# Choosing the two experts of a token on VectorE: thirteen pieces of one operation instead of six pieces of two or three

## The chip, the core and the metric

One core of a Trainium2 chip. The metric is the device time of one execution in microseconds (us); lower is better. The engines are TensorE (PE; its weight loads are listed as PEld), VectorE (DVE), ScalarE (ACT), GpSimd (POOL) and SyncE (SP, which only issues DMAs). Each engine works through its own instructions in order, and waits for others, or for its own earlier results, on semaphores.

## The reference, cut to what matters

A transformer block on x of shape (4, 1024, 128): layer norm with modulation, attention with 16 heads of 8 features, a gated residual, a second modulated layer norm, and a mixture of 8 experts of which each token uses two, with another gated residual. The part that the change touches is the choice of the two experts:

```python
logits = jax.nn.silu(xt @ rw1 + rb1) @ rw2 + rb2
_, idx = jax.lax.top_k(logits, K)                     # K = 2 of E = 8
mask = jnp.zeros((n, E), bool).at[jnp.arange(n)[:, None], idx].set(True)
w = jax.nn.softmax(jnp.where(mask, logits, -jnp.inf), axis=1)
```

## The kernel before, in words

Three stages follow one another: `prepare` (first norm, q, k, v), `attend` (attention of all four sequences, and beside it the routing of the first three) and `mix` (the experts, and beside them the routing of the last sequence). Each is a block that all engines enter and leave together.

`attend` runs 256 steps, 64 for each sequence: 4 groups of 4 heads, 16 steps each, one step for 128 keys against 512 queries. Softmax subtracts the row maximum, so the scores are computed twice. In each step PE makes two *maximum units* (`max_scores`, L711: two products of 128x512 into one of two PSUM buffers `ps_max`); DVE reduces each unit to its row maxima (`take_max`, L902), and PE may write unit n only when unit n-2 has been reduced. PE also makes four score tiles (L732) which ACT turns into probabilities (L832), and adds the probabilities' products with v (`add_ctx`, L747, two halves per step). PE's order in a step is: first half of `add_ctx`, two score tiles, second half, first unit, two score tiles, second unit, then what else is due (`beside`). Every 8 steps DVE joins the maxima of a half group (`row_max`, L910), ACT copies the finished context (L837), PE transposes it (L768) and ACT copies it again (L844), and DVE inverts the sums (L917).

The routing of sequence b is laid out by hand over the 64 steps of the next sequence: `route_time(s)` gives b and the step n, and `ROUTE_AT` the steps of PE's and ACT's parts (the logits at n = 34 and 36, the counting matmul at 45). On DVE, `route_piece(s, place)` runs behind each unit of the step, at position `at = 2n + place`; below, a unit is named by that position (unit 75 is the second one of n = 37). The choice starts behind unit 75. It works on small tiles (128 partitions, 8 token tiles, 8 experts: 64 elements a partition): add the bias; then twice (n = 0, 1): maximum over the experts (`top`), which experts equal it (`cand[0]`), times a table of descending numbers (`cand[1]`), maximum of that (`first`), the one that equals it (`chosen`); in between the first choice is pushed down to -3e38 (`left`). At the end `both`, the sum of the two masks, for PE's counting matmul, and `gap`, the difference of the two maxima, for the weights.

Each operation but the last two goes through `link`: the operation raises a semaphore when it has finished, and DVE waits for it before it goes on.

```python
def link(ins):
    ins.then_inc(step, 1)
    dve.wait_ge(step, steps.more())
```

In `mix` DVE makes the same choice for the last sequence behind expert tiles 18 and 19. It copies there the weights of a tile (L1572) and adds the bias to its result (L1578).

Of the kernel before, what the change touches and what calls it, by code (L numbers as in the profile page):

```python
# [22 lines left out]
ALU = mybir.AluOpType  # L23
ACT = mybir.ActivationFunctionType
AX = mybir.AxisListType
# [53 lines left out]
W_UP, W_B1, W_B2, W_END = 0, HID, HID + HC, HID + HC + D  # L79
assert CLEARS * CLEAR == SLOT_TILES  # L80
PAD = 4
ROUTE = ("ctx0", "ctx1", "proj0", "proj1", "turn0", "turn1", "router0", "router1", "logits0", "logits1", "counts")


# [442 lines left out]
def attend(nc, t, k):  # L527
    with ExitStack() as ctx:
# [40 lines left out]
        r = route_buffers(k["routing"], sb, "_attend", spare[0], spare[1].rearrange("p (t d) -> p t d", d=D))  # L569
# [327 lines left out]
        @block.vector  # L897
        def _(dve):
            def take_max(n):
                g, u, tile, c = n // UNITS, n // 2 % 2, n % UNITS // 4, n % 2  # L900
                dve.wait_ge(max_scores_ready, n + 1)
                dve.reduce_max(half_max[tile // HT % 2][:, c, 2 * u:2 * u + 2, tile % HT],  # L902
                               ps_max[n % 2][:].rearrange("p (r n) -> p r n", r=2), axis=AX.X).then_inc(max_taken, 1)

            def join_halves(h):

                dve.wait_ge(max_taken, HALF_UNITS * (h + 1))
                if h:
                    dve.wait_ge(max_parts_ready, h)
                dve.tensor_tensor(row_max[:], half_max[h % 2][:, 0], half_max[h % 2][:, 1],  # L910
                                  ALU.max).then_inc(row_max_ready, 1)

            def invert_sums(chunk):

                dve.wait_ge(slot_taken, SLOT["turned", chunk] + 1)
                view = turned[chunk % 2][:].rearrange("p (t c) -> p t c", c=32)
                dve.reciprocal(inv_sum[chunk % 2][:], view[:, :, HD]).then_inc(sums_inverted, 1)  # L917

            def step(s):
                for place, n in enumerate(units(s)):  # L920
                    if n is not None:
                        take_max(n)
                    route_piece(s, place)
                if s and (chunk := turned_in(s - 1)) is not None:
                    invert_sums(chunk)
                if (h := split_in(s)) is not None:
                    join_halves(h)

            def route_piece(s, place):

                b, n = route_time(s)
                if not 0 <= b < EARLY:
                    return
                at = 2 * n + place
                if 26 <= at < 26 + NT:
                    route.stats(b, at - 26)
                if at == 26 + NT:
                    route.variance(b)
                if 75 <= at < 81:
                    if at == 75:  # L940
                        dve.wait_ge(slot_taken, SLOT["logits1", b] + 1)
                        if b:
                            dve.wait_ge(r.slot_ready, b)
                    route.choice(at - 75)
                if at == 98 and b == EARLY - 1:
                    dve.wait_ge(r.slot_ready, EARLY)
                    route.tiles(0)

            route = route_on_dve(dve, k, r)
            for n in range(HALF_UNITS):  # L950
                take_max(n)
            join_halves(0)
            for n in range(HALF_UNITS, HALF_UNITS + LEAD):
                take_max(n)
            join_halves(1)
            dve.wait_ge(r.tables_ready, r.TABLES)
            for s in range(ALL_STEPS):
                step(s)
            invert_sums(CHUNKS - 1)
# [10 lines left out]
def routing(nc, ctx, k):  # L970
# [25 lines left out]
    r.fold4, r.fold2 = sb("fold4", [P, 2, NT, NE // 2]), sb("fold2", [P, 2, NT, NE // 4])  # L996
    r.both = sb("both", [P, PAD + NT, NE])
    r.top = [sb(f"top{i}", [P, NT]) for i in range(2)]
# [250 lines left out]
def route_on_dve(dve, k, r):  # L1249

    step, steps = r.dve_step, r.dve_steps
# [5 lines that stand above are left out]
# [14 lines left out]
    wide = [P, NT, NE]  # L1271

    def over_e(v):
        return v[:].unsqueeze(2).to_broadcast(wide)

    def add_bias():
        link(dve.tensor_tensor(r.logit[:], r.logit_in[:], r.rb2[:].unsqueeze(1).to_broadcast(wide), ALU.add))

    def top(n):
        of = r.logit if n == 0 else r.left  # L1280
        link(dve.tensor_reduce(r.top[n][:], of[:], axis=AX.X, op=ALU.max))
        link(dve.tensor_tensor(r.cand[0][:], of[:], over_e(r.top[n]), ALU.is_equal))

    def first_of(n):

        link(dve.tensor_tensor(r.cand[1][:], r.cand[0][:], r.order[:].unsqueeze(1).to_broadcast(wide), ALU.mult))
        link(dve.tensor_reduce(r.first[n][:], r.cand[1][:], axis=AX.X, op=ALU.max))

    def choose(n):
        link(dve.tensor_tensor(r.chosen[:, n], r.cand[1][:], over_e(r.first[n]), ALU.is_equal))  # L1290
        if n == 0:
            link(dve.scalar_tensor_tensor(out=r.left[:], in0=r.chosen[:, 0], scalar=-3e38, in1=r.logit[:],
                                          op0=ALU.mult, op1=ALU.add))

    def both():
        dve.tensor_tensor(r.both[:, PAD:, :], r.chosen[:, 0], r.chosen[:, 1], ALU.add).then_inc(r.both_ready, 1)
        dve.tensor_tensor(r.gap[:], r.top[0][:], r.top[1][:], ALU.subtract).then_inc(r.gap_ready, 1)

    def choice(piece):

        n, part = divmod(piece, 3)
        if part == 0:
            if n == 0:
                add_bias()
            top(n)
        if part == 1:
            first_of(n)
        if part == 2:
            choose(n)
            if n == 1:  # L1310
                both()

    def tiles(stage):

# [23 lines left out]
        dve.tensor_scalar(r.expert[:, at:at + n], r.expert_f[:, 0:n], float(NE - 1), None,  # L1338
                          ALU.min).then_inc(r.tiles_ready, 1)

    made = Steps()
    made.choice = choice
    made.stats = stats
    made.variance = variance
    made.tiles = tiles
    return made


def route_on_pe(pe, k, r):
# [48 lines left out]
def mix(nc, t, k):  # L1398
# [5 lines left out]
    with ExitStack() as ctx:  # L1404
# [40 lines left out]
        r = route_buffers(k["routing"], sb, "_mix")  # L1445
# [114 lines left out]
        def _(dve):  # L1560
# [73 lines left out]
            for n in range(ALL_TILES):  # L1634
                later = n + WRING - 1
                add_bias(n)
                if later < ALL_TILES:
                    copy_w(later, e)
                if later + 1 < ALL_TILES:
                    e = expert(later + 1)  # L1640
                if n == 3:
                    dve.wait_ge(route_taken, ROUTE.index("proj1") + 1)
                    late.gate(LATE)
                if n == 4:
                    late.residual(LATE)
                if n == 5:
                    for tile in range(NT):
                        route.stats(LATE, tile)
                if n == 6:
                    route.variance(LATE)  # L1650
                if n in (8, 9):
                    late.norm(LATE, n - 8)
                if n == 10:
                    late.modulate(LATE)
                if n == 11:
                    late.shift(LATE)
                if n == 16:
                    late.update(LATE)
                if n == 18:
                    dve.wait_ge(route_taken, ROUTE.index("logits1") + 1)  # L1660
                    for piece in range(3):
                        route.choice(piece)
                if n == 19:
                    for piece in range(3, 6):
                        route.choice(piece)
                if n == 22:
                    dve.wait_ge(route_taken, ROUTE.index("counts") + 1)
                    places.slots(LATE, 1)
                if n == 24:
                    places.weights(LATE)  # L1670
                if n == 26:
                    route.tiles(1)
                for b, at in enumerate(COMBINE_AT):
                    if n == at:
                        weigh(b, 0, whole)
                    if n == at + 1:
                        weigh(b, 1, whole)
                    if n == at + 2:
                        add_choices(b, whole)
                    if n == at + 3:  # L1680
                        gate_sum(b, whole)
                    if n == at + 4:
                        add_to_x(b, whole, 2)
                if n in (GATED_AT, GATED_AT + 1):
                    gate_weight(n - GATED_AT)
            for half in range(2):
                part = slice(half * NT // 2, (half + 1) * NT // 2)
# [107 lines left out]
```

## Time and profile before

| | |
|---|---|
| median of 3 runs | 989.49 us (988.11 to 991.61) |
| the profiled execution | 991.75 us; its span 989.9 us |
| DVE busy | 779.0 us (79% of the span) |
| L902 alone | 596.3 us, 512 units of 1216 ns |
| ACT busy | 760.6 us (77%); L832 553.8 us |
| PE busy | 869.6 us (88%), granted clock 0.947 over the span |

The busy times of a page are an average over the three stages. Matmul ends are modelled, so PE's 88% doesn't say that PE is the limit. In `attend`, DVE, ACT and PE are all close to full, and which of them is waited for changes from step to step.

### The profile page before, as it was taken

The numbers are of one execution on the slowest core, as the hardware profiler recorded it, in microseconds if no ns is written. First come the engines' busy times: TensorE is split into PE (matmuls) and PEld (weight loads), VectorE is DVE, ScalarE is ACT, GpSimd is POOL, SyncE is SP. The second block draws the span as 40 slices with busy tenths as digits, with TensorE's granted clock in tenths as the row PEclk, the third lists the DMA queues.
The fourth block names the chain that finished last, engine by engine and source line by source line (L and its number), as shares of the span: only waits on it lengthen the run. The fifth ranks groups of instructions, "written<-read, shape, count | busy, mean of one in ns | idle before, by whom it ended". The sixth has DMA issues, their size and how long they took to land. (4 is left out here: it accounts for less than half of the span.)

```text
span 989.9 us, 22083 instructions
## 1 busy us (share of the span) xinstructions
PE 869.6 (88%) x7998; PEld 398.6 (40%) x7998; DVE 779.0 (79%) x1058; ACT 760.6 (77%) x1636; POOL 347.8 (35%) x649
## 2 busy tenths in 40 slices
PE   6554799999999999899999989999998869998991
PEld 3230133333333233233323323332332259998991
DVE  6949799999998988998898899989886117643385
ACT  5550399999999888899988889998888946665660
POOL 6522000000003352161235216133522616477573
PEclk9775599999999999999999999999999979999996
DMA  5672041441431010171001001100000112123553
GB/s 141 242 278 84 1 147 37 145 176 34 146 115 47 20 34 2 34 225 45 16 20 34 2 33 37 42 19 17 2 2 2 45 47 61 55 69 83 147 139 88
DMA packets 60394, 72.06 MB, mean 73 GB/s; under 512 B 9949, under 2 KB 42212, under 8 KB 60288
## 3 DMA queue, kind: packets, MB, share of 16 engines
q1 hardware_dynamic: 55456, 61.82, 19.3%
q0 software_dynamic: 4544, 8.44, 2.6%
q8 instruction: 66, 1.08, 0.5%
q10 hardware_dynamic: 288, 0.40, 0.1%
q14 instruction: 40, 0.33, 0.1%
HBM read 30.08 MB, written 41.06 MB: 72 GB/s over the span
## 5 line engine op out<-in xcount | busy, mean ns | idle before, releaser
L902 DVE TENSOR_REDUCE half_max<-ps_max 128x2 f32<-128x1024 f32 x512 | 596.3, 1216 | 62.2 <-PE ps_max L711 61.1
L832 ACT ACTIVATE probs<-ps_scores 128x512 f32<-128x512 f32 x1024 | 553.8, 596 | 71.8 <-PE ps_scores L732 57.5
L747 PE MATMUL ps_ctx<-probs,v_grp 128*32 128x256 f32 x4096 | 328.7, 393 | 13.2 <-ACT probs L832 12.4
L711 PE MATMUL ps_max<-k_set,q_set 48*128 48x512 bf16 x1024 | 207.4, 400 | 36.4 <-DVE half_max L902 29.3
L732 PE MATMUL ps_scores<-q_set,k_set 51*128 51x512 bf16 x1024 | 206.5, 386 | 0.7 <-DMA q_set<-max_rows 0.5
L747 PEld LDWEIGHTS ps_ctx<-probs,v_grp 128*32 128x32 f32 x4096 | 80.8, 108 | 141.2 <-issue 71.9
L711 PEld LDWEIGHTS ps_max<-k_set,q_set 48*128 48x128 bf16 x1024 | 49.9, 94 | 191.7 <-DVE half_max L902 105.7
L732 PEld LDWEIGHTS ps_scores<-q_set,k_set 51*128 51x128 bf16 x1024 | 73.1, 93 | 134.0 <-ACT probs L832 94.2
L1541 ACT ACTIVATE hid<-ps_up,w_tile 128x128 f32<-128x128 f32 x312 | 89.2, 368 | 48.1 <-PE ps_up L1708 48.0
L1509 POOL DMA_INDIRECT y_rows<-y,slots_in x78 | 90.0, 1154 | 64.6 <-DVE y L1578 48.7
L638 POOL CAST max_parts<-row_max 128x16 bf16<-128x16 f32 x32 | 6.3, 197 | 297.4 <-DVE row_max L910 297.1
L1708 PE MATMUL ps_up<-slots_t,w_tile 128*128 128x128 f32 x624 | 84.7, 280 | 2.3 <-DVE w_tile L1572 2.3
L1718 PE MATMUL ps_down<-w_down,hid 128*128 x624 | 83.0, 276 | 0.4 <-DVE y L1578 0.4
L1578 DVE TENSOR_TENSOR y<-ps_down,w_tile 128x128 f32<-128x128 f32 x78 | 22.7, 290 | 73.3 <-PE ps_down L1718 63.2
L1708 PEld LDWEIGHTS ps_up<-slots_t,w_tile 128*128 128x128 f32 x624 | 77.5, 195 | 3.6 <-DVE w_tile L1572 2.8
L1718 PEld LDWEIGHTS ps_down<-w_down,hid 128*128 128x128 f32 x624 | 75.9, 192 | 0.7 <-issue 0.6
L1145 POOL DMA_INDIRECT slots<-h,slot x64 | 62.9, 983 | 19.6 <-issue 16.2
L630 POOL TENSOR_TENSOR ctx<-turned,inv_sum 128x128 f32<-128x128 f32 x32 | 13.0, 406 | 126.1 <-DVE inv_sum L917 126.1
L1572 DVE COPY w_tile<-w_all 128x644 f32 x78 | 39.3, 504 | 6.5 <-issue 6.3
L1702 PE MATMUL ps_slots_t<-ident,slots_in 128*128 128x128 f32 x78 | 22.0, 283 | 13.5 <-DMA slots_in<-slots 13.5
L1536 ACT COPY slots_t<-ps_slots_t 128x128 f32<-128x128 f32 x78 | 21.8, 280 | 13.9 <-PE ps_slots_t L1702 13.9
L851 ACT COPY max_rows<-ps_scores 48x128 bf16<-48x128 bf16 x32 | 8.0, 251 | 25.8 <-PE ps_scores L760 25.8
(200 smaller groups left out, 625.7 us busy)
## 6 DMA issues: line engine op xcount, KB each, us to landing
slots<-zero_rows SPq DMA_DIRECT2D x43, 387.0 KB, 5.2
q_terms<-parts SPq DMA_DIRECT2D x24, 256.0 KB, 2.8
k_terms<-parts SPq DMA_DIRECT2D x24, 256.0 KB, 3.2
q_set<-q_terms SPq DMA_DIRECT2D x32, 192.0 KB
k_set<-k_terms SPq DMA_DIRECT2D x32, 192.0 KB
slots_in<-slots SPq DMA_DIRECT2D x78, 64.5 KB, 1.8
rows<-y_rows SPq DMA_DIRECT2D x16, 256.0 KB, 5.1
q_set<-max_rows SPq DMA_DIRECT2D x128, 3.0 KB
```

The source lines that it names most:

```text
L711: ins = pe.matmul(ps_max[n % 2][:, r * BANK:(r + 1) * BANK], q_set[g % SETS][rows, u, tile * P:(tile + 1) * P], k_set[g % SETS][rows, u, c ...
L732: pe.matmul(bank[:], k_set[g % SETS][operand, u, tile * P:(tile + 1) * P], q_set[g % SETS][operand, u, c * BANK:(c + 1) * BANK], start=Tru ...
L747: ins = pe.matmul(ps_ctx[32 * head:32 * head + 32, columns], v_grp[g % 2][:, tile, head, :], probs[:, s % RING, head, columns], start=tile ...
L832: act.activation(probs[:, s % RING, place, :], ps_scores[n % BANKS_S][:], ACT.Exp, scale=float(HD) ** -0.5).then_inc(slot_taken, 1)
L902: dve.reduce_max(half_max[tile // HT % 2][:, c, 2 * u:2 * u + 2, tile % HT], ps_max[n % 2][:].rearrange("p (r n) -> p r n", r=2), axis=AX. ...
L1145: pool.indirect_dma_start(k["slots"], bass.IndirectOffsetOnAxis(r.slot[:, b, n, i:i + 1], axis=0), r.h[:, i, :], None).then_inc(r.scattere ...
L1509: pool.indirect_dma_start(k["y_rows"], bass.IndirectOffsetOnAxis(to, axis=0), y[n % YRING][:], None, bounds_check=Y_ROWS - 1, oob_is_err=F ...
L1541: ins = act.activation(hid[n % 2][:, c, :], ps_up[n % 2][:, c * P:(c + 1) * P], ACT.Silu, bias=w_tile[n % WRING][:, W_B1 + c:W_B1 + c + 1])
L1572: dve.tensor_copy(w_tile[n % WRING][:], w_all[:, e, :]).then_inc(w_ready, 1)
L1578: dve.tensor_tensor(y[n % YRING][:], ps_down[n % 2][:, 0:D], w_tile[n % WRING][:, W_B2:W_END], ALU.add).then_inc(y_ready, 1)
L1708: ins = pe.matmul(ps_up[n % 2][:, c * P:(c + 1) * P], w_tile[n % WRING][:, c * P:(c + 1) * P], slots_t[n % 2][:], start=True, stop=True)
L1718: ins = pe.matmul(ps_down[n % 2][:, 0:D], hid[n % 2][:, c, :], w_down[:, e, c, :], start=c == 0, stop=c == HC - 1)
```

## The change

The choice becomes thirteen pieces, at positions 75 to 87. Each is one operation (the last has two), and the wait for an operation's result stands ahead of the next piece instead of right behind the operation. The result of each operation and their order are the same. In `mix` the first six pieces go behind tile 18 and the other seven behind tile 19, so that `left` moves from the former to the latter.

```diff
+CHOICES = 13
...
-                if 75 <= at < 81:
+                if 75 <= at < 75 + CHOICES:
...
-    def add_bias():
-        link(dve.tensor_tensor(r.logit[:], r.logit_in[:], r.rb2[:].unsqueeze(1).to_broadcast(wide), ALU.add))
-
-    def top(n):
+    def made(ins):
+
+        ins.then_inc(step, 1)
+        steps.more()
+
+    def choice(piece):
+
+        dve.wait_ge(step, steps.seen)
+        if piece == 0:
+            made(dve.tensor_tensor(r.logit[:], r.logit_in[:], r.rb2[:].unsqueeze(1).to_broadcast(wide), ALU.add))
+            return
+        n, part = divmod(piece - 1, 6)
         of = r.logit if n == 0 else r.left
-        link(dve.tensor_reduce(r.top[n][:], of[:], axis=AX.X, op=ALU.max))
-        link(dve.tensor_tensor(r.cand[0][:], of[:], over_e(r.top[n]), ALU.is_equal))
...
+        if part == 0:
+            made(dve.tensor_reduce(r.top[n][:], of[:], axis=AX.X, op=ALU.max))
+        if part == 1:
+            made(dve.tensor_tensor(r.cand[0][:], of[:], over_e(r.top[n]), ALU.is_equal))
+        if part == 2:
+            made(dve.tensor_tensor(r.cand[1][:], r.cand[0][:], r.order[:].unsqueeze(1).to_broadcast(wide), ALU.mult))
+        if part == 3:
+            made(dve.tensor_reduce(r.first[n][:], r.cand[1][:], axis=AX.X, op=ALU.max))
+        if part == 4:
+            made(dve.tensor_tensor(r.chosen[:, n], r.cand[1][:], over_e(r.first[n]), ALU.is_equal))
+        if part == 5 and n == 0:
+            made(dve.scalar_tensor_tensor(out=r.left[:], in0=r.chosen[:, 0], scalar=-3e38, in1=r.logit[:],
                                           op0=ALU.mult, op1=ALU.add))
...
+        if part == 5 and n == 1:
+            dve.tensor_tensor(r.both[:, PAD:, :], r.chosen[:, 0], r.chosen[:, 1], ALU.add).then_inc(r.both_ready, 1)
+            dve.tensor_tensor(r.gap[:], r.top[0][:], r.top[1][:], ALU.subtract).then_inc(r.gap_ready, 1)
...
-                    for piece in range(3):
+                    for piece in range(CHOICES // 2):
                         route.choice(piece)
                 if n == 19:
-                    for piece in range(3, 6):
+                    for piece in range(CHOICES // 2, CHOICES):
                         route.choice(piece)
```

On DVE, from the first operation of the choice of sequence 0 on, with what each instruction waits for (`route_dve_step` is the semaphore of `link`, `max_scores_ready` says that PE has filled a unit); before:

```order
L902 TENSOR_REDUCE half_max<-ps_max 128x2 [waits max_scores_ready] x4
L1277 TENSOR_TENSOR logit<-logit_in,rb 128x64 [waits score_slot_taken]
L1281 TENSOR_REDUCE top<-logit 128x8 [waits route_dve_step]
L1282 TENSOR_TENSOR cand<-logit,top 128x64 [waits route_dve_step]
L917 RECIPROCAL inv_sum<-turned 128x16 [waits score_slot_taken,route_dve_step]
L902 TENSOR_REDUCE half_max<-ps_max 128x2 [waits max_scores_ready]
L1286 TENSOR_TENSOR cand<-cand,order 128x64
L1287 TENSOR_REDUCE first<-cand 128x8 [waits route_dve_step]
L902 TENSOR_REDUCE half_max<-ps_max 128x2 [waits max_scores_ready,route_dve_step]
```

and at the same place in the changed kernel (its lines are numbered one or more higher):

```order
L903 TENSOR_REDUCE half_max<-ps_max 128x2 [waits max_scores_ready] x4
L1286 TENSOR_TENSOR logit<-logit_in,rb 128x64 [waits route_dve_step,score_slot_taken]
L918 RECIPROCAL inv_sum<-turned 128x16 [waits score_slot_taken]
L903 TENSOR_REDUCE half_max<-ps_max 128x2 [waits max_scores_ready]
L1291 TENSOR_REDUCE top<-logit 128x8 [waits route_dve_step]
L903 TENSOR_REDUCE half_max<-ps_max 128x2 [waits max_scores_ready]
L1293 TENSOR_TENSOR cand<-logit,top 128x64 [waits route_dve_step]
```

The units and the reciprocal no longer wait for an operation of the choice, and between an operation and the one that needs its result there now stands a unit. At the end of the same choice on DVE, before:

```order
L1290 TENSOR_TENSOR chosen<-cand,first 128x64
L1296 TENSOR_TENSOR both<-chosen 128x64 [waits route_dve_step]
L1297 TENSOR_TENSOR gap<-top 128x8
L902 TENSOR_REDUCE half_max<-ps_max 128x2 [waits max_scores_ready] x7
L910 TENSOR_TENSOR row_max<-half_max 128x16 [waits max_parts_ready,max_taken]
```

and in the changed kernel:

```order
L1299 TENSOR_TENSOR chosen<-cand,first 128x64 [waits route_dve_step]
L903 TENSOR_REDUCE half_max<-ps_max 128x2 [waits max_scores_ready]
L1304 TENSOR_TENSOR both<-chosen 128x64 [waits route_dve_step]
L1305 TENSOR_TENSOR gap<-top 128x8
L911 TENSOR_TENSOR row_max<-half_max 128x16 [waits max_parts_ready,max_taken]
```

The seven units that stood between the choice and the joining of the maxima (units 81 to 87) now stand between the choice's last operations, and `both` is made seven units later.

## Rows read from the trace of the kernel before

**Rows 1.** Busy time by window (columns named in the first line): choice group, regular group.

```profile
core 0: us, PE busy (x) PEld busy (x) DVE busy (x) ACT busy (x) POOL busy (x), PEclk, DMA share, GB/s
387.40:411.10 23.70, 20.59 (x210) 7.04 (x208) 21.60 (x34) 18.88 (x38) 1.24 (x5) 1.00 0.04 12
...
140.00:159.80 19.80, 19.46 (x203) 6.21 (x200) 18.80 (x19) 18.55 (x37) 1.25 (x5) 1.00 0.22 70
```

**Rows 2.** Timeline of DVE, choice of sequence 0: start us, us, instruction, [idle before].

```profile
391.59 2.36 DVE L902 TENSOR_REDUCE half_max<-ps_max 128x2 f32<-128x1024 f32 x2 [1.45 <-PE ps_max L711]
393.86 0.21 DVE L1277 TENSOR_TENSOR logit<-logit_in,rb 128x64 f32<-128x64 f32 x1
394.11 0.22 DVE L1281 TENSOR_REDUCE top<-logit 128x8 f32<-128x64 f32 x1
...
396.37 1.23 DVE L902 TENSOR_REDUCE half_max<-ps_max 128x2 f32<-128x1024 f32 x1
...
402.69 0.22 DVE L1296 TENSOR_TENSOR both<-chosen 128x64 f32<-128x64 f32 x1
402.84 0.16 DVE L1297 TENSOR_TENSOR gap<-top 128x8 f32<-128x8 f32 x1
402.91 8.11 DVE L902 TENSOR_REDUCE half_max<-ps_max 128x2 f32<-128x1024 f32 x7
411.06 0.17 DVE L910 TENSOR_TENSOR row_max<-half_max 128x16 f32<-128x16 f32 x1
411.40 2.35 DVE L902 TENSOR_REDUCE half_max<-ps_max 128x2 f32<-128x1024 f32 x2 [0.17 <-PE ps_max L711]
414.20 2.36 DVE L902 TENSOR_REDUCE half_max<-ps_max 128x2 f32<-128x1024 f32 x2 [0.45 <-PE ps_max L711]
```

**Rows 3.** Timeline of DVE: first operation and row_max of the other two choices.

```profile
567.24 0.22 DVE L1277 TENSOR_TENSOR logit<-logit_in,rb 128x64 f32<-128x64 f32 x1
...
584.44 0.17 DVE L910 TENSOR_TENSOR row_max<-half_max 128x16 f32<-128x16 f32 x1
...
740.01 0.22 DVE L1277 TENSOR_TENSOR logit<-logit_in,rb 128x64 f32<-128x64 f32 x1
...
757.20 0.18 DVE L910 TENSOR_TENSOR row_max<-half_max 128x16 f32<-128x16 f32 x1
```

**Rows 4.** Timeline of ACT beside the first choice: first and last of six waits.

```profile
395.32 1.08 ACT L832 ACTIVATE probs<-ps_scores 128x512 f32<-128x512 f32 x2 [0.22 <-PE ps_scores L732]
...
405.50 2.86 ACT L832 ACTIVATE probs<-ps_scores 128x512 f32<-128x512 f32 x5 [1.05 <-PE ps_scores L732]
```

**Rows 5.** Timeline of PE beside the first choice.

```profile
404.19 0.39 PE L711 MATMUL ps_max<-k_set,q_set 48*128 48x512 bf16 x2 [0.86 <-DVE half_max L902]
...
408.81 0.10 PEld L711 LDWEIGHTS ps_max<-k_set,q_set 48*128 48x128 bf16 x2 [0.31 <-DVE half_max L902]
...
409.50 0.64 PE L747 MATMUL ps_ctx<-probs,v_grp 128*32 128x256 f32 x8 [0.30 <-ACT probs L832]
```

**Rows 6.** Timeline of DVE: statistics, one operation behind each unit, without a wait.

```profile
326.30 0.28 DVE L1261 BATCH_NORM_STATS2 stats<-x_sb 128x6 f32<-128x128 f32 x1
326.50 0.23 DVE L917 RECIPROCAL inv_sum<-turned 128x16 f32<-128x16 f32 x1
...
327.73 0.28 DVE L1261 BATCH_NORM_STATS2 stats<-x_sb 128x6 f32<-128x128 f32 x1
...
334.34 0.28 DVE L1261 BATCH_NORM_STATS2 stats<-x_sb 128x6 f32<-128x128 f32 x1
```

**Rows 7.** Timelines of PE, ACT and SP: from the last counts to the stage mix.

```profile
760.59 0.43 PE L1364 MATMUL ps_scores<-both,before 128*128 128x96 f32 x2 [0.19 <-ACT probs L832]
...
792.79 0.59 ACT L844 COPY turned<-ps_scores 128x512 f32<-128x512 f32 x1 [0.81 <-PE ps_scores L768]
...
799.50 6.26 SPq L1466 DMA_DIRECT2D slots_in<-slots  x6
```

**Rows 8.** Timelines of DVE and PE in mix: last choice and its reader.

```profile
853.83 0.22 DVE L1296 TENSOR_TENSOR both<-chosen 128x64 f32<-128x64 f32 x1
...
854.67 0.36 PE L1364 MATMUL ps_route<-both,before 128*128 128x96 f32 x2
```

More of the change, by code:

```diff
@@ L1274, in over_e @@
         return v[:].unsqueeze(2).to_broadcast(wide)
-    def add_bias():
-        link(dve.tensor_tensor(r.logit[:], r.logit_in[:], r.rb2[:].unsqueeze(1).to_broadcast(wide), ALU.add))
-    def top(n):
-        of = r.logit if n == 0 else r.left
-        link(dve.tensor_reduce(r.top[n][:], of[:], axis=AX.X, op=ALU.max))
-        link(dve.tensor_tensor(r.cand[0][:], of[:], over_e(r.top[n]), ALU.is_equal))
-    def first_of(n):
-        link(dve.tensor_tensor(r.cand[1][:], r.cand[0][:], r.order[:].unsqueeze(1).to_broadcast(wide), ALU.mult))
-        link(dve.tensor_reduce(r.first[n][:], r.cand[1][:], axis=AX.X, op=ALU.max))
@@ L1289, in choose @@
[L1289 to L1292, printed above, removed]
-                                          op0=ALU.mult, op1=ALU.add))
-    def both():
-        dve.tensor_tensor(r.both[:, PAD:, :], r.chosen[:, 0], r.chosen[:, 1], ALU.add).then_inc(r.both_ready, 1)
-        dve.tensor_tensor(r.gap[:], r.top[0][:], r.top[1][:], ALU.subtract).then_inc(r.gap_ready, 1)
@@ L1299, in choice @@
[L1299 to L1311, printed above, removed]
+    def made(ins):
[7 more added lines that the diff above has]
+        n, part = divmod(piece - 1, 6)
+        of = r.logit if n == 0 else r.left
+        if part == 0:
[10 more added lines that the diff above has]
+            made(dve.scalar_tensor_tensor(out=r.left[:], in0=r.chosen[:, 0], scalar=-3e38, in1=r.logit[:],
+                                          op0=ALU.mult, op1=ALU.add))
+        if part == 5 and n == 1:
+            dve.tensor_tensor(r.both[:, PAD:, :], r.chosen[:, 0], r.chosen[:, 1], ALU.add).then_inc(r.both_ready, 1)
+            dve.tensor_tensor(r.gap[:], r.top[0][:], r.top[1][:], ALU.subtract).then_inc(r.gap_ready, 1)
@@ L1339, in tiles @@
                           ALU.min).then_inc(r.tiles_ready, 1)
[L1341 to L1346, printed above, removed]
+    pieces = Steps()
+    pieces.choice = choice
+    pieces.stats = stats
+    pieces.variance = variance
+    pieces.tiles = tiles
+    return pieces
 def route_on_pe(pe, k, r):
```

## The prediction, made before the run

> **What bounds the kernel now.** I first compared windows. The group of 8 steps in which the choice of sequence 0 lies takes 23.70 us between two joinings of the maxima, a group without routing 19.80. ACT does almost the same work in both, 18.88 and 18.55 us, and has 4.82 us free in the one against 1.25 in the other; DVE does 21.60 against 18.80 [rows 1]. So in this group ACT waits, and the question is for whom. On DVE's timeline there is no idle time from the start of unit 74 at 391.59 to row_max at 411.06 [rows 2]: DVE is what everything stands behind. ACT waits six times for scores from 395.32 to 405.50, at first 0.22 us and at the end 1.05 [rows 4], and PE, which makes those scores, is itself held by DVE's reductions: 0.86 us ahead of the unit at 404.19, 0.31 (on the weight load) at 408.81 [rows 5]. That last one is unit 87, which may be written when unit 85 has been reduced. From there it changes hands: at 409.50 PE waits 0.30 us for ACT [rows 5], and units 88 and 90 find DVE idle for 0.17 and 0.45 us [rows 2]. What the choice costs the kernel is thus what it adds to DVE up to the end of unit 85. The other two choices in this stage look the same: from the first operation to row_max 17.20 us in all three [rows 2, 3].
>
> **The end of unit 85 before.** Units 81 to 87 follow without an operation between them: 8.11 us with a last one of 1.23, so one starts every (8.11 - 1.23) / 6 = 1.147 us [rows 2]. Unit 85 starts at 402.91 + 4 x 1.147 = 407.50 and ends at 408.73. Unit 90 starts at 414.20, 5.47 us later, over PE and ACT.
>
> **What the change does to it.** Before, all 14 operations stand ahead of unit 85; after, ten of them do, each behind a unit of its own. Let p be what one such operation adds to the time between two units, and 0.10 what the reciprocal of this place adds (with it the step from one statistics operation to the next is 327.73 - 326.30 = 1.43, without it (334.34 - 327.73) / 5 = 1.322 [rows 6]). Then unit 76 starts at 393.86 + p + 0.10, unit 85 nine times (1.147 + p) later, and it ends 1.23 later: 405.51 + 10p. The gain there is 3.22 - 10p per choice.
>
> **The price p.** With a wait behind it an operation of the choice takes 0.25 us from start to start (393.86 to 394.11 [rows 2]). The change takes that wait off: its predecessor has finished a unit earlier when it is issued, and the unit behind it needs nothing of it. The trace has two rows for an operation that nothing waits for: `both`, of the same 64 elements, lets `gap` start 0.15 us after it [rows 2], and the statistics (128 elements), one behind each unit as the choice will be, add 1.322 - 1.147 = 0.175 [rows 6]. I take 0.16, between them, since the size is that of the first and the place that of the second. The bounds: below, 0.07, which `gap` (8 elements) costs before the next unit; above, 0.25, as if the waits had cost nothing. Gains per choice: 1.62 at 0.16; 2.52 and 0.72 at the bounds.
>
> A satisfied wait itself I cost at nothing: the reciprocal waits for ACT's semaphore and still starts 0.20 us behind a statistics operation of 0.28 us [rows 6].
>
> The Trainium skill speaks against this term. Its page "VectorE: DVE Perf Modes", section "The DRAIN you can't avoid", says that the next VectorE operation can't issue until the pipe is empty, and that eight copies with a semaphore after each took as long as eight with one at the end: the semaphore costs nothing extra. By that p would stay 0.25 and the gain 0.72 per choice. Here `gap` starts 0.15 us behind an operation that lasts 0.22 [rows 2], so the trace doesn't bear it out for operations this short; I keep it as a rival.
>
> **Where the gain goes next.** Behind unit 85 two chains compete for unit 90. Over PE and ACT it comes 5.47 us after the end of unit 85, as before: 405.51 + 1.6 + 5.47 = 412.58. Over DVE there are units 86 and 87, now with an operation behind each, and row_max: with `both` and `gap` (0.07) it starts at 393.86 + 13p + 0.10 + 12 x 1.147 + 0.07 = 407.79 + 13p = 409.87; 0.17 more to unit 88 (0.34 less the idle 0.17 [rows 2]) and two units of 1.147 give 412.33. PE's chain is later by 0.25, so the four operations behind unit 85 lie in the 0.62 us that DVE stood idle there (0.17 + 0.45 [rows 2]) and in what is saved, and unit 90 comes 1.62 us earlier. ACT can follow: it needs 18.88 us in the group and had 4.82 free [rows 1].
>
> For the third choice no units follow 87; PE and ACT go on alone, and start 1.62 us earlier too. `both` is later by seven units, but at most at row_max's old place, 757.20 [rows 3]; the counting matmul came at 760.59 [rows 7] and moves up by the gain, so 1.8 us stay between them. For the first two, PE can't reach the counting matmul (n = 45) before unit 89 has been reduced, behind `both`.
>
> From there on nothing runs to a clock: the last turned context at 792.79 and the first load of experts at 799.50 [rows 7] follow in a chain and move together. In `mix` the choice has the same 14 operations back to back, every wait still on the path; only `left` changes sides of a tile. It ends at the same 853.83 + 0.22, and PE reads `both` at 854.67 [rows 8]; without these 0.6 us each further 0.1 us there would be 0.1 us of PE's. I count nothing.
>
> **Sum.** 3 x 1.62 = 4.9 us. The profiled execution (span 989.9, its own time 991.75, which is 2.3 above the median of the runs) would take 986.9; the median 989.49 - 4.9 = **984.6 us**, 0.5% less.
>
> **The rivals.**
> 1. *The waits were free.* p stays 0.25, only the order has changed. PE's chain gives 3 x 0.72 = 2.2 us, DVE's chain to unit 90 0.70 per choice, about the same: **987.3**. For it, the skill's rule; against it, the 0.15 and 0.175 us above.
> 2. *PE and ACT take only part.* A step at DVE's new pace lasts 2 x (1.147 + 0.16) = 2.61 us, and PE's own way from unit 85's end to unit 88 holds two halves of `add_ctx` of 0.64 [rows 5] and a score pair. If ACT's waits don't shrink with DVE's pace, half of the gain remains: **987.0**. For it, the 0.30 us that PE already waits for ACT at 409.50 [rows 5]; against it, ACT's 4.82 us.
> 3. *Slower: thirteen interruptions cost more than six.* If an operation of this kind between two units costs more than anything shown, since each breaks the run of units, DVE's chain passes PE's. Unit 90 over DVE is at 410.25 + 13p, which passes 414.20 at p = 0.30. At p = 0.45 it is 1.9 us later in two choices, and unit 85 of the third 1.3: 5.1 us more, **994.6**. For it, that the units read PSUM and the operations SBUF, in turns; against it, the statistics, in turns too, at 0.175.
>
> **How the numbers follow.** Forecast 0.70, first rival 0.15, second 0.10, third 0.05. Up to p = 0.22 the forecast is over 0.3% (3.0 us, about what a measurement of this kernel tells from no change); I leave 0.04 of its 0.70 within. The first two rivals lie within 0.3%, with a little over the edge. So faster 0.67, same 0.28, slower 0.05. The range: downwards p = 0.07 gives 3 x 2.52 = 7.6 us, 981.9; upwards the first two rivals at 987.3 and, with runs that spread by 1.75 us to either side of their middle, something more. I take 982.3 to 988.0.
>
> **What the new profile would show.** Right: an operation behind each of units 75 to 87, 1.29 to 1.32 us from one unit to the next; from the first operation to row_max 16.0 us in place of 17.20; ACT's six waits smaller; the group of 23.6 us shorter by 1.1 to row_max and by 1.6 to unit 90; `mix` as it was, 4.9 us earlier. Wrong: 1.40 us from unit to unit (first rival), DVE idle between units 76 and 87 for PE (second), row_max later than 17.2 us after the first operation (third), or PE waiting for `both`. The prediction would also fail if `mix` changed by some us by itself, which the step-by-step sum can't see.

## The result, and the profile after

The changed kernel takes 984.02 us (median of 20 runs, 981.51 to 989.0), the kernel before in the same sessions 990.54 (20 runs, 988.11 to 994.47): a ratio of 0.9937, with a 95% interval of 0.9923 to 0.995. That is 6.5 us, where 4.9 was forecast.

The same two windows as in [rows 1], here of the changed kernel: the group with the choice of sequence 0, and a group without routing (us; busy time and instructions of PE, PEld, DVE, ACT, POOL; clock; DMA).

```profile
385.60:407.48 21.88, 21.08 (x211) 7.25 (x211) 20.27 (x32) 19.18 (x38) 1.24 (x5) 1.00 0.06 15
138.22:157.94 19.72, 19.38 (x199) 6.12 (x198) 18.76 (x18) 18.46 (x37) 1.24 (x5) 1.00 0.19 63
```

The windows of [rows 1] reach 0.04 us beyond both ends of their groups. The group with the choice began there with

```profile
387.44 0.18 DVE L910 TENSOR_TENSOR row_max<-half_max 128x16 f32<-128x16 f32 x1
```

and lasted 23.62 us to the next row_max at 411.06 [rows 2]. It is now 1.74 us shorter, and the group without routing is 19.72 us in both kernels. DVE is busy for 1.28 us less in it (21.55 before) with the same operations.

DVE's timeline of this choice, which answers to [rows 2] (start us, us, instruction, idle before):

```profile
389.75 2.36 DVE L903 TENSOR_REDUCE half_max<-ps_max 128x2 f32<-128x1024 f32 x2 [1.44 <-PE ps_max L712]
392.02 0.21 DVE L1286 TENSOR_TENSOR logit<-logit_in,rb 128x64 f32<-128x64 f32 x1
392.15 0.25 DVE L918 RECIPROCAL inv_sum<-turned 128x16 f32<-128x16 f32 x1
392.31 1.17 DVE L903 TENSOR_REDUCE half_max<-ps_max 128x2 f32<-128x1024 f32 x1
393.39 0.20 DVE L1291 TENSOR_REDUCE top<-logit 128x8 f32<-128x64 f32 x1
393.51 1.22 DVE L903 TENSOR_REDUCE half_max<-ps_max 128x2 f32<-128x1024 f32 x1
394.64 0.22 DVE L1293 TENSOR_TENSOR cand<-logit,top 128x64 f32<-128x64 f32 x1
...
406.01 0.22 DVE L1299 TENSOR_TENSOR chosen<-cand,first 128x64 f32<-128x64 f32 x1
406.14 1.23 DVE L903 TENSOR_REDUCE half_max<-ps_max 128x2 f32<-128x1024 f32 x1
407.27 0.22 DVE L1304 TENSOR_TENSOR both<-chosen 128x64 f32<-128x64 f32 x1
407.40 0.17 DVE L1305 TENSOR_TENSOR gap<-top 128x8 f32<-128x8 f32 x1
407.48 0.18 DVE L911 TENSOR_TENSOR row_max<-half_max 128x16 f32<-128x16 f32 x1
407.56 2.36 DVE L903 TENSOR_REDUCE half_max<-ps_max 128x2 f32<-128x1024 f32 x2
410.22 2.36 DVE L903 TENSOR_REDUCE half_max<-ps_max 128x2 f32<-128x1024 f32 x2 [0.30 <-PE ps_max L712]
```

From `cand` behind unit 77 to `chosen` behind unit 86 there are nine units with an operation each: (406.01 - 394.64) / 9 = 1.263 us. An operation therefore adds p = 1.263 - 1.147 = 0.116 us; 0.16 had been put down. From the first operation to row_max it is 15.46 us (17.20 before), to unit 90 18.20 (20.34 before [rows 2]): 2.14 us gained. Unit 88 no longer waits, unit 90 waits 0.30 us for PE.

ACT beside this choice, of which [rows 4] show the waits before:

```profile
393.48 2.19 ACT L833 ACTIVATE probs<-ps_scores 128x512 f32<-128x512 f32 x4 [0.22 <-PE ps_scores L733]
...
396.27 2.19 ACT L833 ACTIVATE probs<-ps_scores 128x512 f32<-128x512 f32 x4 [0.46 <-PE ps_scores L733]
398.63 2.19 ACT L833 ACTIVATE probs<-ps_scores 128x512 f32<-128x512 f32 x4 [0.17 <-PE ps_scores L733]
401.16 2.19 ACT L833 ACTIVATE probs<-ps_scores 128x512 f32<-128x512 f32 x4 [0.33 <-PE ps_scores L733]
403.68 0.60 ACT L833 ACTIVATE probs<-ps_scores 128x512 f32<-128x512 f32 x1 [0.33 <-PE ps_scores L733]
```

Its waits are 1.51 us in sum. The six before made 3.59 us, up to 1.05 for one; one of them, 0.51 us, was for the row maxima that PE had transposed (L760) and not for scores. The copy of the context follows at 404.28 without a wait.

The end of the third choice, on DVE, PE and SP, answers to [rows 3, 7]:

```profile
734.55 0.21 DVE L1286 TENSOR_TENSOR logit<-logit_in,rb 128x64 f32<-128x64 f32 x1
...
749.80 0.23 DVE L1304 TENSOR_TENSOR both<-chosen 128x64 f32<-128x64 f32 x1
...
752.89 0.43 PE L1358 MATMUL ps_scores<-both,before 128*128 128x96 f32 x2 [0.19 <-ACT probs L833]
...
791.80 13.96 SPq L1460 DMA_DIRECT2D slots_in<-slots  x13
```

From its first operation to the first load of the experts' stage it took 59.49 us before and takes 57.25 now. `both` stands 3.1 us ahead of the matmul that reads it, which still waits 0.19 us, for ACT. The stage `mix` is unchanged: from that load to the end of the span it was 989.9 - 799.50 = 190.4 us and is 981.9 - 791.80 = 190.1.

### The profile page after: what moved, and what is told of

Its sections match the earlier page's. It is cut to its first block and busy times, and to the rows that moved or that the text cites. A ratio compares the mean times of both kernels' runs of the same rounds, so it can differ in the third digit from the quotient of the medians.

```text
span 981.9 us, 22070 instructions
## 1 busy us (share of the span) xinstructions
PE 866.1 (88%) x7998; PEld 397.9 (41%) x7998; DVE 775.1 (79%) x1058; ACT 760.2 (77%) x1636; POOL 346.7 (35%) x649
```

## The experiments

All ratios are to the kernel before, run on the same chip in the same session. Times to unit 90 are of the choice of sequence 0, from its first operation (20.34 us before, 18.20 with the change).

### Thirteen pieces, the wait behind the operation again

```diff
     def made(ins):
 
         ins.then_inc(step, 1)
-        steps.more()
+        dve.wait_ge(step, steps.more())
```

> The thirteen pieces as in the change, but each operation waited for right behind it again, as before the change. If the wait is what an operation of the choice costs (0.25 us from start to start instead of the 0.13 that the changed kernel shows), a unit with its operation takes about 1.39 us instead of 1.26, the first operation to row_max takes 17.2 us instead of 15.46, and only 3.22 - 2.5 = 0.7 us a choice is gained over the kernel before: about 2.2 us in all, 988.3. If the semaphores cost nothing and the gain comes from the new places alone, the units stay at 1.26 us and the time is that of the changed kernel, about 984.

Measured: 990.52 us against 991.49, ratio 0.9984 (0.9971 to 0.9997). DVE's timeline:

```profile
394.20 0.21 DVE L1286 TENSOR_TENSOR logit<-logit_in,rb 128x64 f32<-128x64 f32 x1
...
397.07 0.21 DVE L1293 TENSOR_TENSOR cand<-logit,top 128x64 f32<-128x64 f32 x1
397.32 1.23 DVE L903 TENSOR_REDUCE half_max<-ps_max 128x2 f32<-128x1024 f32 x1
398.46 0.21 DVE L1295 TENSOR_TENSOR cand<-cand,order 128x64 f32<-128x64 f32 x1
...
411.17 0.17 DVE L911 TENSOR_TENSOR row_max<-half_max 128x16 f32<-128x16 f32 x1
411.25 2.35 DVE L903 TENSOR_REDUCE half_max<-ps_max 128x2 f32<-128x1024 f32 x2
413.90 2.36 DVE L903 TENSOR_REDUCE half_max<-ps_max 128x2 f32<-128x1024 f32 x2 [0.30 <-PE ps_max L712]
```

The unit starts 0.25 us behind `cand` instead of 0.13, and a unit with its operation takes 1.39 us. To row_max it is 16.97 us, to unit 90 19.70: 0.64 us gained, where 0.7 was expected. Spreading by itself is worth less than a third of the 2.14. Only 0.23 of it lies ahead of row_max (17.20 us before); most of the rest is idle time behind it, where DVE waited 0.17 and 0.45 us for PE before [rows 2] and waits 0.30 here. The medians differ by 1.0 us where 2.2 was expected; the interval of the ratio, 0.3 to 2.9 us, holds both.

### Six pieces at the old places, the wait ahead of the operation

```diff
+GROUPED = ((0, 1, 2), (3, 4), (5, 6), (7, 8), (9, 10), (11, 12))
...
-                if 75 <= at < 75 + CHOICES:
+                if 75 <= at < 81:
...
-                    route.choice(at - 75)
+                    for piece in GROUPED[at - 75]:
+                        route.choice(piece)
```

> Six pieces of two or three operations at the old places, but each operation waits for its predecessor only when it is issued itself. Five of the twelve waits then lie behind a unit and seven remain inside the pieces. If a wait costs 0.25 - 0.13 = 0.12 us, a choice gets 0.6 us shorter up to unit 81, and the kernel is 1.8 us faster than before, 988.7; row_max comes 16.6 us after the first operation. If the gain of the change comes from the places alone, nothing changes: 990.5, 17.2 us.

Measured: 989.58 us, ratio 0.9975 (0.9959 to 0.9992). DVE's timeline:

```profile
395.93 0.21 DVE L1301 TENSOR_TENSOR chosen<-cand,first 128x64 f32<-128x64 f32 x1
396.18 0.23 DVE L1303 SCALAR_TENSOR_TENSOR left<-chosen,logit 128x64 f32<-128x64 f32 x1
396.32 1.22 DVE L904 TENSOR_REDUCE half_max<-ps_max 128x2 f32<-128x1024 f32 x1
...
409.11 0.18 DVE L912 TENSOR_TENSOR row_max<-half_max 128x16 f32<-128x16 f32 x1
409.45 2.36 DVE L904 TENSOR_REDUCE half_max<-ps_max 128x2 f32<-128x1024 f32 x2 [0.17 <-PE ps_max L713]
412.25 2.36 DVE L904 TENSOR_REDUCE half_max<-ps_max 128x2 f32<-128x1024 f32 x2 [0.45 <-PE ps_max L713]
```

Both prices stand side by side here: inside the piece `left` starts 0.25 us behind `chosen`, whose result it needs; the unit starts 0.14 us behind `left`, of which it needs nothing. The first operation is at 392.53, so unit 90 comes after 19.72 us: 0.62 gained, 0.6 expected. A wait is worth 0.12 us, but at the old places only five of twelve can be taken off.

### One more operation behind each of twelve pieces

```diff
...
                     route.choice(at - 75)
+                    if at - 75 < CHOICES - 1:
+                        route.idle(at - 75)
...
+    def idle(piece):
+        dve.tensor_tensor(r.idle[:, piece], r.order[:].unsqueeze(1).to_broadcast(wide), r.rb2[:].unsqueeze(1).to_broadcast(wide), ALU.add)
...
```

> The changed kernel with one more operation of the same size, which nothing needs, behind each of the first twelve pieces. If VectorE's time up to unit 85 sets the group, each adds the 0.13 us that both takes ahead of gap: 1.3 us a choice up to unit 85 and 1.6 up to row_max, the kernel 3.9 us slower than the changed one, about 988. If TensorE and ScalarE set the pace there, as the second rival of the prediction has it, the additions disappear in waiting and the time stays near 984.

Measured: 989.62 us, ratio 0.9987 (0.9974 to 1.0); the changed kernel has 0.9937. DVE's timeline:

```profile
395.02 0.21 DVE L1289 TENSOR_TENSOR logit<-logit_in,rb 128x64 f32<-128x64 f32 x1
...
410.51 0.21 DVE L1302 TENSOR_TENSOR chosen<-cand,first 128x64 f32<-128x64 f32 x1
410.64 0.22 DVE L1311 TENSOR_TENSOR idle<-order,rb 128x64 f32<-128x64 f32 x1
410.78 1.22 DVE L904 TENSOR_REDUCE half_max<-ps_max 128x2 f32<-128x1024 f32 x1
411.91 0.22 DVE L1307 TENSOR_TENSOR both<-chosen 128x64 f32<-128x64 f32 x1
...
414.85 2.36 DVE L904 TENSOR_REDUCE half_max<-ps_max 128x2 f32<-128x1024 f32 x2 [0.30 <-PE ps_max L713]
```

Unit 90 comes after 19.83 us, 1.63 later than with the change: all twelve additions of 0.136 us arrive there, though unit 90 still waits 0.30 us for PE. DVE sets the group after the change as before; ACT and PE don't swallow any of it. By the ratios the kernel is some 5 us slower than the changed one, where 3.9 was expected. All twelve, not the ten up to unit 85, count; this is taken up below.

### The change again, beside three further versions

> The changed kernel itself, on the same chip as the three that follow. From the first operation of a choice to the second row_max behind it 35.2 us, 2.1 less than before, in all three choices; in time 6.5 us under the kernel before. The group in which the experts' weights are loaded (row_max to row_max) took 20.33 us before and 20.96 after the change, 21.24, 21.22 and 20.81 in the three experiments: if that is chance of the transfers, it lies anywhere in that range here; if the change lengthens it, it is at 20.9 or more again.

Measured: 986.09 us against 992.5, ratio 0.9943 (0.9927 to 0.996). The first choice again takes 35.21 us to the second row_max (391.57 to 426.78). The group of the weights' loads lasts 20.18 us this time, less than before the change: its length varies with the transfers from one execution to the next, and a longer one isn't shown to come with the change.

### Six operations of the choice on GpSimd

```diff
+SHARED = (1, 2, 4, 5, 7, 8, 10, 11)
...
-                    route.choice(at - 75)
+                    if at - 75 in SHARED:
+                        route.shared_choice(at - 75, b)
...
+    done(pool.tensor_tensor(r.logit[:], r.logit_in[:], r.rb2[:].unsqueeze(1).to_broadcast(wide), ALU.add))
+    pool.wait_ge(r.choice_dve, 8 * b + 2)
+    done(pool.tensor_tensor(r.cand[1][:], r.cand[0][:], order, ALU.mult))
+    pool.wait_ge(r.choice_dve, 8 * b + 4)
+    done(pool.tensor_scalar(r.left[:], r.chosen[:, 0], -3e38, None, ALU.mult))
+    pool.wait_ge(r.choice_pool, made + 3)
+    done(pool.tensor_tensor(r.left[:], r.left[:], r.logit[:], ALU.add))
...
```

> The changed kernel with the bias, the two products with the table, the pushing down of the first choice, both and gap on GpSimd in the attention stage, which waits there for row_max anyway; VectorE keeps eight operations, each behind a unit of its own. If VectorE's time still sets the group, four operations fewer ahead of the end of unit 85 are worth 4 x 0.12 = 0.5 us a choice, 1.4 us in all, about 982.6 where the changed kernel has 984. If TensorE and ScalarE have become the limit after the change, or VectorE has to wait for GpSimd, nothing is gained or some tenths are lost.

Measured: 983.26 us, ratio 0.991 (0.9892 to 0.9928), beside 0.9943 for the change on the same chip. DVE's timeline, then POOL's:

```profile
391.15 2.36 DVE L907 TENSOR_REDUCE half_max<-ps_max 128x2 f32<-128x1024 f32 x2 [1.45 <-PE ps_max L716]
...
394.66 0.20 DVE L1343 TENSOR_REDUCE top<-logit 128x8 f32<-128x64 f32 x1
...
411.14 2.36 DVE L907 TENSOR_REDUCE half_max<-ps_max 128x2 f32<-128x1024 f32 x2 [0.41 <-PE ps_max L716]
```

```profile
394.11 0.32 POOL L1264 TENSOR_TENSOR logit<-logit_in,rb 128x64 f32<-128x64 f32 x1
396.21 0.32 POOL L1266 TENSOR_TENSOR cand<-cand,order 128x64 f32<-128x64 f32 x1 [1.78 <-DVE cand L1345]
...
407.19 0.32 POOL L1275 TENSOR_TENSOR both<-chosen 128x64 f32<-128x64 f32 x1 [3.17 <-DVE chosen L1350]
```

From unit 74 to unit 90 it takes 19.99 us here, 410.22 - 389.75 = 20.47 with the change and 22.61 before [rows 2]: another 0.48 a choice, as expected. In this choice DVE never waits for POOL in between. POOL takes 0.32 us for an operation, more than DVE, in time that it had spent waiting. The 2.8 us between the two medians are more than the 1.4 that the timelines explain; the rest lies within the spread of the runs, a few us for each kernel.

### The loads of the experts' weights in two groups, and both edits

```diff
-                if g == 8:
-                    load_weights()
+                if g in (8, 9):
+                    load_weights(g - 8)
...
-                for e in range(NE):
+                for e in range((0, 2, NE)[part], (2, NE, NE)[part]):
```

> The changed kernel with the loads of the experts' weights given out in two groups, two experts' in the old one and six in the next. TensorE waited 0.48 us before the change and 1.10 after it for the row maxima that SyncE sends behind these 18 loads. If that queue is what lengthens the group, it comes down from 20.96 to the 19.7 of the others and the kernel gains about 1 us over the changed one; the next group may take over part of the wait, since six experts' loads are ahead of its row maxima. If the wait comes from transfers in general, the group stays at 20.3 to 21.2.

Measured: 984.38 us, ratio 0.992 (0.9904 to 0.9937). The median is 1.7 us below that of the repetition, 986.09, with intervals that overlap. The group of the loads lasts 19.73 us, and the next 20.86, as it did with the change (448.19 to 469.04, 20.85). But the version with the shared choice, whose loads were left alone, shows 19.73 too. PE's wait there, of the kernel before, of the changed one and of its repetition:

```profile
446.72 0.39 PE L732 MATMUL ps_scores<-q_set,k_set 51*128 51x512 bf16 x2 [0.48 <-DMA q_set<-max_rows]
```

```profile
443.36 0.39 PE L733 MATMUL ps_scores<-q_set,k_set 51*128 51x512 bf16 x2 [1.10 <-DMA q_set<-max_rows]
```

```profile
442.13 0.39 PE L733 MATMUL ps_scores<-q_set,k_set 51*128 51x512 bf16 x2 [0.32 <-DMA q_set<-max_rows]
```

It varies from run to run of the same kernel. Of the seven traces without the split, six show this wait, of 0.32 to 1.38 us, and that of the shared choice shows none; the two with the split show none either. So these traces don't tell whether the split took it away. This stays open.

Both edits, the shared choice and the loads in two groups, in one kernel:

> Both of the preceding edits together. If their causes are separate, the gains add: 1.4 and 1 us under the changed kernel, about 981.6; if one of them does nothing, the other's gain is left.

Measured: 982.82 us, ratio 0.9899 (0.9881 to 0.9917), the fastest of all versions. Its choice is that of the shared version (unit 90 at 411.12) and its group of loads 19.73 us. The interval overlaps that of the shared choice alone; that the second edit adds anything isn't shown.

## Why the prediction was right, step by step

**What bounds the kernel.** Right: DVE's time in the choice. Three edits that change nothing but DVE's instructions (the first three experiments) moved unit 90 by 0.64, 0.62 and, the other way, 1.63 us, and the extra operations arrived in full.

**The price p.** Right in kind, too large in size: 0.16 was forecast, 0.116 measured. This is the mis-sized term. The two rows it came from were for a larger operation (0.175) and for `both` with `gap` behind it (0.15, 0.13 in the new timeline); behind a unit, the operation starts 1.13 us after the unit, where a next unit would start after 1.147, and the next unit 0.13 after the operation. With 0.116 the predicted formula gives 3.22 - 1.16 = 2.06 us a choice and 6.2 in all; measured were 2.14 to unit 90 in the first choice and 59.49 - 57.25 = 2.24 to the load in the third. The signs of the new profile are off by the same term: 1.29 to 1.32 us from unit to unit were forecast and 1.263 measured, 16.0 us to row_max and 15.46 measured. The group was to be 1.1 us shorter to row_max, by the prediction's own formula 1.2; it is 1.74.

**Two effects that need each other.** The prediction had both in one formula; what the places alone bring is there as the price of its first rival, 0.72 us. Spreading alone gives 0.64, waiting late alone 0.62, together 2.14. Late waiting removes only those waits behind which an independent instruction stands; spreading puts one behind all twelve. 12 x 0.12 + 0.64 = 2.08, where 2.14 was measured.

**Where the gain goes next.** Right that PE, not DVE, comes last at unit 90 (0.25 us was worked out, 0.30 measured). One step of it was off: I let PE's chain start at unit 85. In all four kernels with thirteen full pieces unit 90 starts 2.85 us after the end of unit 87: 410.22 - 407.37 with the change, 413.90 - 411.05 with the wait behind, 414.85 - 412.00 with the extra operations, and the repetition the same. Unit 89 may be written when 87 has been reduced, and PE goes on from there. In the version with the wait behind, PE waits for DVE ahead of unit 89 and then for nothing up to unit 90:

```profile
409.82 1.23 DVE L903 TENSOR_REDUCE half_max<-ps_max 128x2 f32<-128x1024 f32 x1
...
411.10 0.39 PE L712 MATMUL ps_max<-k_set,q_set 48*128 48x512 bf16 x2 [0.39 <-DVE half_max L903]
...
413.47 0.39 PE L712 MATMUL ps_max<-k_set,q_set 48*128 48x512 bf16 x2
```

This is why twelve additions counted and not ten. For the change itself both chains give the same within 0.1 us.

**`both`, `mix`, the end.** Right: `both` was 3.1 us early, where at least 1.8 had been worked out, `mix` took 190.1 us in place of 190.4.

**The rivals.** The first, waits that cost nothing, falls: the same thirteen pieces with the wait behind take 1.39 us a unit, with the wait ahead 1.26. That was the rule of the Trainium skill's page "VectorE: DVE Perf Modes", section "The DRAIN you can't avoid"; for operations of 64 elements between reductions these runs don't agree with it, 0.25 against 0.13 us from start to start. A later section of the same page, "Two Vector instructions with no wait between them", lets an instruction that is not held start before its predecessor has finished, and that is what the timelines show: with the change `gap` starts at 407.40, 0.09 us before `both` has ended (407.27 + 0.22). The second rival, PE and ACT taking half, falls with the extra operations. The third, dear interruptions, falls with p = 0.116.

**The sum.** In the two traces the way from the first operation of the first choice to the first load is 405.64 us before and 399.78 after, 5.9 less, although the loads' group took 0.63 more (20.96, before 20.33); in the repetition it is 398.97, 6.7 less. Without that group the gains add up: 2.14 and 2.13 us to the second row_max of the first two choices and 2.24 to the load in the third, 6.5 in all. The medians differ by 6.5 too. That 984.6 came within 0.6 us of the 984.0 measured is in part luck: the 989.49 it started from, a median of 3 runs, lies 1.05 below that of 20, and the gain was put 1.6 too small. The spans of the two profiled executions differ by 8.0; 1.84 of that stands ahead of the first choice (393.86 - 392.02) and is no part of the change: the experiments, whose code is the same up to there, reach their first operation at 391.57 to 395.02.

## What to carry to other kernels

A chain of small dependent operations on the engine that sets the pace cost here about as much in waits on itself (0.12 us each) as in work (0.116 us each). Put an independent instruction of the bulk work between each two, and move the wait from behind the producer to ahead of the consumer: each of the two alone brought 0.6 us here, both 2.1. To find out whether the engine really sets the pace, add the same work once more and see if it arrives in full. Here it did, and four operations fewer ahead of unit 87 then brought 0.48 of the expected 0.5 us. How much more can be taken away this doesn't tell: unit 90 waits 0.41 us for PE in the shared version, 0.30 with the change, and PE's row in the group with the choice already reads 21.08 of 21.88 us, with modelled ends.

## What the hardware showed that had not been expected

A VectorE operation of 128x64 fp32 between two PSUM reductions of 1.23 us adds only 0.116 us, though its own row reads 0.21 to 0.22; a wait for it by the next instruction adds 0.12 more, about doubling it. The joining of the maxima hides two operations nearly whole. It waits for the last reduction, and used to start 1.27 us after that one had started (0.04 after it had ended, 411.02 to 411.06 [rows 2]); with `both` and `gap` in between it starts 1.34 us after (406.14 to 407.48), so the two add 0.07 us. The next unit, which came 0.34 us after row_max and waited there for PE [rows 2], follows it after 0.08 us now that PE has it ready.
